# Attention's results laid by DMA in rows per dimension and divided there, in a kernel of sixteen samples

## The reference, cut to what matters

```python
# x: 16 samples x 1024 tokens x 256
left = layernorm(x)[..., :128]
q, k, v = (left @ W.T).reshape(16, 1024, 16 heads, 8) for Wq, Wk, Wv
att = softmax(q . k / 4, over keys)
out = (att @ v).reshape(16, 1024, 128) @ Wo.T + bo
x = x + layernorm(out)
h = layernorm(x)
gf = global_net(mean of h over tokens)          # three small layers
for _ in range(3):                              # three cycles
    tf = sigmoid(gelu(gelu(gelu(h@w1+b1)@w2+b2)@w3+b3)@w4+b4)      # 256-256-128-64-1
    coupling = 0.1 + adaptive_range * (0.7*gf + 0.3*tf - 0.5) * 2
    h = h + coupling * twist(h)
x = x + layernorm(h)
```

## Time and profile before

| | us |
|---|---|
| median of 3 runs (lowest, highest) | 3556.51 (3555.34, 3559.84) |
| the profiled execution's own time | 3557.75 |
| its span in the profile | 3555.8 |
| busy: PE / DVE / ACT / POOL | 3379.5 / 2981.2 / 2931.5 / 972.2 |
| granted TensorE clock, mean | 0.975 of full speed |

### The profile page before, as it was taken

One profiled execution on the slowest core, in us unless ns is written; L12 is line 12 of the kernel. 1 busy time (PEld: TensorE's weight loads), 2 busy tenths in 40 slices (PEclk: granted clock), 3 DMA queues, 4 the chain that ended last, 5 costly groups with the idle time before them and its releaser, 6 DMA issues.

```text
span 3555.8 us, 56168 instructions
## 1 busy us (share of the span) xinstructions
PE 3379.5 (95%) x19968; PEld 1008.8 (28%) x19968; DVE 2981.2 (84%) x5677; ACT 2931.5 (82%) x3868; POOL 972.2 (27%) x1353
## 2 busy tenths in 40 slices
PE   4999999999999999999999999999999999999996
PEld 1222232323324232232323224232232323223232
DVE  5998989888898988989888897988989888898821
ACT  2767979798897979889798897979889797896974
POOL 3002050421505133060421405033050422404034
PEclk6998999999999999999999999999999999999998
DMA  3101102021211202111020211202111020211001
GB/s 85 27 24 44 33 30 34 26 54 23 51 26 33 54 18 55 30 45 32 26 54 22 51 37 27 49 26 46 30 48 28 26 55 22 44 32 26 3 24 36
DMA packets 71957, 127.89 MB, mean 36 GB/s; under 512 B 37120, under 2 KB 38528, under 8 KB 63616
## 3 DMA queue, kind: packets, MB, share of 16 engines
q1 hardware_dynamic: 68896, 106.75, 12.8%
q0 software_dynamic: 2304, 16.78, 2.6%
q10 hardware_dynamic: 480, 0.79, 0.1%
HBM read 34.61 MB, written 33.55 MB: 19 GB/s over the span
## 4 chain that ended last, share of the span: by engine, by line
PE 72%; DVE 10%; ACT 9%; issue 4%; POOL 2%; DMA 0%; SPq 0%; ACTq 0%; POOLq 0%; DVEq 0%
PE heads_ps L424 24%; PE ring_ps L391 15%; PE scoresT_ps L409 11%; PE scoresT_ps L521 10%; DVE max_parts L814 8%; ACT p_sb L599 4%; PE scoresT_ps L526 3%; DVE stats L825 1%; ACT headsT L608 1%; PE ring_ps L453 1%; PE scoresT_ps L529 1%; PE scoresT_ps L532 1%; POOL y_sb L985 1%; PE scoresT_ps L391 1%; POOL couple L1008 1%
## 5 line engine op out<-in xcount | busy, mean ns | idle before, releaser
L814 DVE TENSOR_REDUCE max_parts<-ring_ps 128x1 f32<-128x512 f32 x3704 | 2343.5, 684 | 269.5 <-PE ring_ps L391 210.5
L599 ACT ACTIVATE p_sb<-scoresT_ps 128x1024 f32<-128x1024 f32 x2048 | 1969.8, 1024 | 103.3 <-PE scoresT_ps L409 79.5
L424 PE MATMUL heads_ps<-p_sb,v_sb 128*9 128x512 f32 x8192 | 1080.4, 599 | 17.9 <-ACT headsT L608 11.9
L391 PE MATMUL ring_ps<-k_rows,q_rows 48*128 48x512 bf16 x3704 | 1074.6, 387 | 17.7 <-DVE max_parts L814 6.3
L409 PE MATMUL scoresT_ps<-q_rows,k_rows 51*128 51x512 bf16 x4096 | 1030.5, 386 | 18.7 <-ACT p_sb L599 9.1
L391 PEld LDWEIGHTS ring_ps<-k_rows,q_rows 48*128 48x128 bf16 x3704 | 263.2, 94 | 1272.6 <-DVE max_parts L814 1177.6
L963 POOL CAST max_wide<-max_all 128x16 bf16<-128x16 f32 x128 | 25.3, 198 | 1709.4 <-DVE max_all L820 1706.7
L521 PE MATMUL scoresT_ps<-state,w 128*128 128x512 f32 x768 | 383.6, 623 | 4.0 <-DVE state L865 2.0
L719 ACT ACTIVATE p_sb<-scoresT_ps,b 128x512 f32<-128x512 f32 x192 | 131.7, 686 | 210.7 <-PE scoresT_ps L521 210.5
L409 PEld LDWEIGHTS scoresT_ps<-q_rows,k_rows 51*128 51x128 bf16 x4096 | 209.4, 94 | 253.4 <-ACT p_sb L599 221.0
L424 PEld LDWEIGHTS heads_ps<-p_sb,v_sb 128*9 128x9 f32 x8192 | 124.5, 88 | 292.1 <-issue 281.6
(11 more groups left out here) (166 smaller groups left out, 2869.5 us busy)
## 6 DMA issues: line engine op xcount, KB each, us to landing
q_rows<-parts SPq DMA_DIRECT2D x378, 64.0 KB
k_rows<-parts SPq DMA_DIRECT2D x378, 64.0 KB
x_sb<-in_x SPq DMA_DIRECT2D x16, 1024.0 KB, 4.8
out<-x_sb SPq DMA_DIRECT2D x16, 1024.0 KB, 3.9
out<-x_in POOLq DMA_DIRECT2D x16, 1024.0 KB, 7.9
x_in<-in_x SPq DMA_DIRECT2D x15, 1024.0 KB, 5.4
q_rows<-max_rows SPq DMA_DIRECT2D x512, 3.0 KB
max_rows<-max_wide SPq DMA_TRANSPOSE x128, 2.3
```

The costliest lines, as they stand in the source:

```text
L391: e.matmul(ring_bank(max_taken, u + 1), q_rows[rows, slot, pair, h * BANK + qb * P:h * BANK + (qb + 1) * P], k_rows[rows, slot, pair, kh * ...
L424: m = e.matmul(heads_ps[32 * j:32 * j + DH + 1, :], v_sb[:, b % 2, kb, 4 * (group % NG) + j, 0:DH + 1], p_sb[:, n % 2, j, :], start=(kb == ...
L599: e.activation(p_sb[:, n % 2, 2 * two:2 * two + 2, :].rearrange("p h n -> p (h n)"), scoresT_ps[:, 2 * two * BANK:(2 * two + 2) * BANK], A ...
L814: e.tensor_reduce(max_parts[:, gi % 2, kh, col:col + 1], bank_of(max_taken, u + 1), AX.X, ALU.max).then_inc(max_taken, 1)
```

## The change

The rows of results are no longer turned. For each group SP sends four DMAs, from the eight rows of each head in `headsT` to eight rows of `feat_h` (one row per dimension of a head, 512 tokens), and with the last group of a half one DMA that gathers its 16 rows of sums to 32 half rows of `sums_in`. The multiplication happens there: VectorE inverts `sums_in` (64x256) in beat 2, SP spreads each inverted row to the eight rows of its head in `sums_h` with two DMAs per half, and VectorE multiplies each half of `feat_h` in place (beats 4 and 5). The rows of Wo are put in the same order on the host. `turn_heads`, `turn_tok`, `take_tok` and `recip` are gone. Most stages get new beats, and one unit moves from the attention steps' allotment to the beats' first (64 to 63 in `BEAT_UNITS`; the steps still end at 192).

```diff
-LAY_AFTER = 3
+SUM_PARTS = 2
+SUM_ROWS = H * SUM_PARTS
+LAID = 16 * (2 * H + NH)
+LAY_AFTER = 6
...
-BEAT_UNITS = (3, 2, 2, 1, 3, 2, 2, 2, 2, 1,
-              2, 2, 2, 3, 3, 2, 2, 4, 2, 1,
-              2, 1, 2, 3, 4, 2, 2, 2, 2, 1)
+BEAT_UNITS = (4, 1, 2, 1, 2, 1, 2, 2, 1, 1,
+              2, 3, 2, 3, 3, 2, 2, 4, 2, 1,
+              2, 1, 2, 3, 4, 2, 2, 2, 3, 1)
...
-LAST_BEAT, LAST_STEP = 28, 0
+LAST_BEAT, LAST_STEP = 27, 1
...
-STATS0, ROOT0, NORM0, TURN_X = (0, 1, 2, 3), 4, (5, 6, 7, 8), (8, 9)
-PROJECT_QK, SPLIT, PROJECT_V = (17, 18, 23, 24), (20, 21, 26, 27), (20, 26)
+STATS0, ROOT0, NORM0, TURN_X = (0, 1, 2, 3), 3, (5, 6, 7, 8), (8, 9)
+PROJECT_QK, SPLIT, PROJECT_V = (17, 18, 23, 24), (20, 21, 26, 27), (22, 29)
-BACK, STATS3, ROOT3, NORM3, ADD_OUT = (10, 11, 12, 13), (11, 12, 13, 14), 15, (17, 18, 19, 25), 27
-HEADS, TURN_TOK, WO, STATS1, ROOT1 = (0, 0, 0, 0, 1, 2, 3, 4), (1, 5), (3, 4, 6, 7), (4, 5, 7, 8), 9
-NORM1, ADD1, STATS2, ROOT2 = (11, 12, 13, 14), (12, 13, 14, 15), (14, 16, 17, 18), 18
-NORM2, STATE = (21, 22, 23, 24), (24, 25, 26, 27)
-GLOBAL = (1, 3, 5)
-TWIST0, UPDATE0, TWIST1, UPDATE1 = 6, 7, 10, 10
+BACK, STATS3, ROOT3, NORM3, ADD_OUT = (8, 9, 10, 11), (10, 11, 12, 13), 14, (16, 17, 20, 24), 26
+INVERT, DIVIDE, WO, STATS1, ROOT1 = 2, (4, 5), (5, 5, 6, 6), (6, 6, 7, 7), 7
+NORM1, ADD1, STATS2, ROOT2 = (10, 11, 12, 13), (11, 12, 13, 15), (14, 16, 17, 18), 19
+NORM2, STATE = (21, 22, 23, 24), (26, 27, 28, 29)
+GLOBAL = (0, 3, 5)
+TWIST0, UPDATE0, TWIST1, UPDATE1 = 6, 7, 9, 10
...
+            def lay_heads(b, group):
+                h, g = divmod(group, NG)
+                e.wait_ge(heads_evac, GROUPS * b + group + 1)
+                if b and group == 0:
+                    e.wait_ge(wo_done, 4 * b)
+                    e.wait_ge(divided, 2 * b)
+                if g == NG - 1:
+                    e.dma_start(sums_in[SUM_ROWS * h:SUM_ROWS * (h + 1), :],
+                                headsT[DH:P:32, h, :, :]).then_inc(heads_laid, 16)
+                for i in range(4):
+                    at = 32 * i + DH * g
+                    e.dma_start(feat_h[at:at + DH, h * BANK:(h + 1) * BANK],
+                                headsT[32 * i:32 * i + DH, h, g, :]).then_inc(heads_laid, 16)
+            def lay_sums(b):
+                e.wait_ge(inverted, b + 1)
+                for h in range(NH):
+                    for k in range(SUM_PARTS):
+                        at = h * BANK + k * BANK // SUM_PARTS
+                        rows = sums_in[SUM_ROWS * h + k:SUM_ROWS * (h + 1):SUM_PARTS, :]
+                        e.dma_start(sums_h[:, at:at + BANK // SUM_PARTS],
+                                    rows.unsqueeze(1).to_broadcast([H, DH, BANK // SUM_PARTS])).then_inc(sums_laid[h], 16)
...
                     if 0 <= b < N - 1 and n < 48:
                         lay_row(b + 1, n)
+                    if valid(b) and n and n % NT == 0:
+                        lay_heads(b, n // NT - 1)
                 for j in range(BEATS):
+                    if valid(b) and j == 0:
+                        lay_heads(b, GROUPS - 1)
+                    if valid(b) and j == INVERT:
+                        lay_sums(b)
...
-            def turn_heads(b, t):
...
-            def turn_tok(b, h):
...
             def project_out(b, j):
-                e.wait_ge(feath_ready, 2 * b + j // 2 + 1)
+                e.wait_ge(divided, 2 * b + j // 2 + 1)
...
             def take_heads(b, n):
                 if b:
-                    e.wait_ge(headT_done, NT * (b - 1) + (group // NG + 1) * TPH)
+                    e.wait_ge(heads_laid, LAID * b)
...
-            def take_tok(b, h):
...
-            def divide(b, t):
...
+            def invert(b):
+                e.wait_ge(heads_laid, LAID * (b + 1))
+                e.reciprocal(sums_in[:, :], sums_in[:, :]).then_inc(inverted, 1)
+            def divide(b, h):
+                half = feat_h[:, h * BANK:(h + 1) * BANK]
+                e.wait_ge(sums_laid[h], 16 * SUM_PARTS * (b + 1))
+                e.tensor_tensor(half, half, sums_h[:, h * BANK:(h + 1) * BANK], ALU.mult).then_inc(divided, 1)
```

More of the change, by code:

```diff
@@ L154, in attention_ffn_program @@
         max_turned, max_rows_laid = sem("max_turned"), sem("max_rows_laid")
+        heads_laid, sums_laid = sem("heads_laid"), [sem(f"sums_laid{h}") for h in range(NH)]
         scores_done, pv_done = sem("scores_done"), sem("pv_done")
@@ L446, in project_v @@
                 m.then_inc(v_done, 1)
-            def turn_heads(b, t):
[L449 to L452, removed]
-                    m = e.transpose(ps[:, g * P:(g + 1) * P], headsT[:, h, g, t % TPH * P:(t % TPH + 1) * P],
-                                    ident[:, :])
-                m.then_inc(headT_done, 1)
-            def turn_tok(b, h):
-                e.wait_ge(divided, NT * b + (h + 1) * TPH)
-                ps = misc_bank(feath_ready, 2 * b + h + 1)
-                for t in range(h * TPH, (h + 1) * TPH):
-                    m = e.transpose(ps[:, t % TPH * P:(t % TPH + 1) * P], tok_h[:, t, :], ident[:, :])
-                m.then_inc(tokT_done, 1)
             def project_out(b, j):
-                e.wait_ge(feath_ready, 2 * b + j // 2 + 1)
+                e.wait_ge(divided, 2 * b + j // 2 + 1)
                 ps = misc_bank(y_taken, 4 * b + j + 1)
@@ L578, in tensor_program @@
                     if valid(b):
-                        if j in TURN_TOK:
-                            turn_tok(b, TURN_TOK.index(j))
-                        for t in range(NT):
-                            if j == HEADS[t]:
-                                turn_heads(b, t)
-                        if j in WO:
-                            project_out(b, WO.index(j))
+                        for i in range(4):
+                            if j == WO[i]:
+                                project_out(b, i)
                         if j in STATE:
@@ L913, in vector_program @@
                     if valid(b):
-                        for t in range(NT):
-                            if j == HEADS[t]:
-                                divide(b, t)
-                        if j in STATS1:
-                            i = STATS1.index(j)
+                        if j == INVERT:
+                            invert(b)
+                        for h in range(NH):
+                            if j == DIVIDE[h]:
+                                divide(b, h)
+                        for i in range(4):
+                            if j != STATS1[i]:
+                                continue
                             e.wait_ge(y_done, 4 * b + i + 1)
@@ L1089, in gpsimd_program @@
                     if valid(b):
-                        if j in WO:
-                            add_bias(b, WO.index(j))
+                        for i in range(4):
+                            if j == WO[i]:
+                                add_bias(b, i)
                         if j == ROOT1:
@@ L1132 @@
     by_side = lambda w: np.ascontiguousarray(w.reshape(2, 4, 2, 8, 128).transpose(4, 2, 0, 3, 1).reshape(128, 128))
+    by_place = lambda w: np.ascontiguousarray(w.T.reshape(4, 4, 8, 256).transpose(1, 0, 2, 3).reshape(128, 256))
     given = {
```

33 lines of the change are left out of this document (8 added, 25 removed).

## The result

| | before | after |
|---|---|---|
| median, us (lowest, highest; 4 runs each) | 3555.93 (3554.51, 3559.84) | 3469.61 (3468.70, 3470.99) |
| span of the profiled execution, us | 3555.8 | 3468.9 |
| granted TensorE clock, mean | 0.975 | 0.980 |

The kernel after is faster by 86.3 us: ratio 0.9756, 95% interval 0.9739 to 0.9773. Forecast were 3503 and a gain of 55. The sign is right and the stated range, 3460 to 3561, held, but only by its lower part: the forecast's own range, 3482 to 3527 (chance 0.47), missed it, and the gain was half as large again.

A forecast was written before the change was run, and what follows sets the result against it. TensorE's queue was taken to bound the beats, with VectorE beside it in the second cycle. Samples 1 to 14 save 4.0 us each (56), sample 15 saves 1, sample 0 loses 2: -55, 3503 us; own range 3482 to 3527, stated 3460 to 3561.

The forecast's parts named there:

- The bound: Beats: first and third cycle last as long as TensorE's queue of work; the second is bounded by TensorE and VectorE.
- The first cycle: First coupling cycle of a full sample: 27.6 us against 30.0, 2.4 less, including 1.5 of waiting before project_out.
- The DMAs on SP: SP's queue in attention: 12.6 us of issuing in 16, so SP keeps up and late maxima cost nothing.
- The second cycle: Second coupling cycle: two transposed tiles and 0.5 to 1 us of VectorE's work gone, 1.4 us less a sample.
- The third cycle: Third coupling cycle: STATE's tiles fill idle time, some 0.3 us given back before the first exp; 0.2 us less.
- The step that failed: Beats and attention of the one sample read: TensorE's clock taken as granted in full.
- One sign of being wrong: Listed sign against the forecast: the granted clock leaves 1.00 between 440 and 3200 us.
- The two ends: Sample 0 without coupling: 2 us lost to the DMA chain; sample 15: 1 us saved; last coupling and tail stay.
- The whole of TensorE's work back: Rival, chance 0.13: copies land in time and old gaps vanish, 5.7 us a sample over 16, 3467.
- VectorE as bound: Rival, chance 0.17: VectorE holds the beats, only its net 1.2 us a sample is saved, 3539.
- Late sums: Rival, chance 0.12: spreading DMAs take 3.4 us each, project_out waits 5 us and 3.5 more, 3603.
- The clock in new gaps: Rival, chance 0.06: TensorE's clock falls behind the new waits, 36 us back, 3539.

The follow-up runs named there:

- e1: Kernel after with 40 unread 128x128 transposes put back on TensorE in the first coupling cycle of each full sample; 3529.36 us, 0.9922 of before.
- e5: Kernel after (new route) with units of maxima and most stages at the places of the kernel before; 3500.17 us, 0.9833 of before.
- e6: Kernel before (old route) with the new places of the stages that do not belong to the heads' route; 3531.33 us, 0.9919 of before.
- e3: Kernel after without the reciprocal and the DMAs spreading the inverted sums, VectorE multiplying each half by itself; 3461.97 us, 0.9730 of before.
- e4: Kernel before with STATE's four tiles at beats 26 to 29 in place of 24 to 27; 3546.95 us, 0.9964 of before.
- e2: Kernel after with a second, unread reciprocal of 64x256 on VectorE right behind the real one; 3478.64 us, 0.9782 of before.
- e7: Kernel after with one more DMA, waited for, between the reciprocal and the spreading of the inverted sums; 3476.63 us, 0.9766 of before.
- e8: Kernel after with three more DMAs in a row between the reciprocal and the spreading of the inverted sums; 3572.14 us, 1.0039 of before.
- e10: Kernel after with first beats' units 3, 2, 2, PROJECT_V's first tile at beat 21 and project_out's last at beat 7; 3468.38 us, 0.9745 of before.
- e12: Kernel after with first units 3, 2, 2, PROJECT_V from beat 21, global network from beat 1, one unit moved from beat 17 to 20; 3446.00 us.

## Why the prediction was right, and where it was off

- **The bound: right for the first cycle.** e1 gave 4.27 us of time for 4.73 of TensorE's work. The removal was forecast at 4.8 a stage before waits; e5 shows 3.8 at the old places, e6 against after 4.45 at the new ones.
- **The first cycle: right in sum, by two errors that cancel.** Forecast 27.6 with 1.5 us of waiting for the DMA chain; measured 27.33 with none. project_out came 14.7 us after the start, not 13.5, and the first half was ready at 13.3 (655.19), not 14.7. TensorE was later mainly because beat 0 took 3.74 us, not 2.9: its fifth unit waits 0.57 for VectorE, which I had not counted (the wait in beat 1, forecast at 0.6, came at 0.46). The chain was faster since the spreading took 3.3 us from the reciprocal's end to the divide, forecast 4.2.
- **The DMAs on SP: right.** Issue 0.63 to 0.69 each (forecast 0.72), the spread ones no dearer than others. The attention steps stayed at 130.05 us (130.03 before at full clock), so nothing there was held up by late maxima.
- **The reciprocal: 1.73 us, forecast 1.8.** The estimate of 2.7 that I made by reading the repeat count of 8 in the Trainium skill ("VectorE: DVE Perf Modes", first budget of the eight-slice walkthrough) as eight passes was too high: the trace has 6.7 ns an element, not 10.4.
- **The second cycle: 1.76 less, forecast 1.4.** Near in size, but I had named two bounds and e5 shows one: 1.7 us less of VectorE's work gave nothing at the old places, and the new places gave 1.7.
- **The third cycle: 0.81 less, forecast 0.2.** This is the mis-sized term: I gave back 0.3 where ScalarE's last state copy stands before the first exp. In fact TensorE's idle time in this cycle went from 1.7 us (25.38 busy of 27.11) to 0.7 (25.56 of 26.29), and the first exp came sooner. All three cycles together saved 5.3 us in a full stage's beats against 4.0: 15 of the missing 32 us (spans).
- **The step that failed: "The clock is granted in full in all of these."** It is true of the one stage that was read. In seven of the twelve full stages of the kernel before the clock fell, at a cost of 11 us, which the prediction put at nothing and which came back. A view of all stages would have shown it. The only rival on the clock stood on the other side, as a loss. One sign of being wrong did show: the clock of the kernel after left 1.00 between 440 and 3200, at 3164 and 3191, in the one stage behind the full ones.
- **The two ends: 8 us more than forecast, in part luck.** For the beats without coupling I forecast 2 us lost to the chain; project_out does wait 3.09 there, but as long without the inversion (e3), and by the first coupling 3.5 were gained. The last coupling and tail, forecast at 1, gave 3.6. How much of either is the change stays open: e4 and the kernel before, alike up to the first exp, reached it 4.5 us apart, and e2's last part is 3.1 us shorter than that of the kernel after with more to do. The two coupling stages beside the twelve saved 6.3 us instead of 8, which takes 2 back.
- **Luck in the number.** The terms 15, 11, 8 and -2 make up the missing 32 us. The 11 belong to no term of the prediction and the 8 to ends whose time varies by itself; the range held them because it had been drawn down past a rival.
- **Rivals.** The whole of TensorE's work back, 3467: the nearest in time, but not by its mechanism, since gaps of 2.6 us a stage remained and 4.3, not 5.7, came back for the transposes. VectorE as bound: refuted by e1 and e3 for the first cycle and by e5 for the second, but e2 shows it 0.8 us away. Late sums: refuted; e7 puts the cover at 1.1 us and e8 shows what the far side would have been, 3572. The clock in new gaps: did not occur in the full stages, and e8 shows that it would have at 4 us.

Open stays what decides whether the clock falls. Waits of 1.2 to 1.6 us within some 4 us were followed by a fall in 7, 5, 8 (before, e4, e5) and 5 (e10) of twelve stages with the same order of work, 0.7 to 0.8 us at the passage in 3 of 132 (eleven kernels at the new places, e6 among them), 4.1 us in all twelve (e8). That the waits are its cause is likely by this count, not shown by a run that changed them alone.

## What to carry to other kernels

Where one engine is busy 95%, cost an edit by that engine's time, then list its gaps by name: most could be filled here by a piece of its own work, and 24 us were left that way (e12), though the one that e10 filled cost more than it held. Measure how much cover a new chain has by adding a hop; it was 1.1 to 1.7 us, and past it a wait of 0.87 us cost 0.4 and one of 4.12 cost 5.7. Read the granted clock over every repetition of a stage, not in one, and compare kernels stage by stage where the ends of the run vary by themselves.

## What the runs showed of the hardware

A DMA from one place in SBUF to another, waited for, takes 1.9 us a hop from issue to the next issue (three in 5.80 us), of which the issue is 0.5 to 0.7. A reciprocal of 64x256 took 1.73 us, a multiply of 128x512 0.69. Behind a short stretch of waits (1.2 to 1.6 us) TensorE's clock stood at its lower level for a few us in some repetitions and not in others with the same gaps, at 1 to 2.5 us each. The same work up to the first exp took 83.5 us in e4 and 88.0 in the kernel before, at a mean granted clock of 0.77 and 0.67.
